# Attention maxima in blocks of 32 queries by 96 keys, with four head groups on the partitions, in a fused attention and expert layer

## The reference

```
q, k, v = split(x @ w_qkv.T)                       # 16 heads of 8 features
scores  = q k^T / sqrt(8)                          # allowed: j <= i and i - j < 64
x1      = layernorm(x + softmax(scores) v @ w_out.T + b_out)
logits  = x1 @ gate_w + gate_b; top 2 of 8 experts, softmax over the two
expert  = silu(((x1 w1 + b1) * (x1 w2 + b2)) wg + bg) w3 + b3
out     = layernorm(x1 + sum over the two of weight * expert(x1))
```

## Time and profile before

| what | value |
|---|---|
| time, median of 3 runs | 330.24 us (330.13 to 331.91) |
| the profiled execution's own time | 330.35 us |
| its span on the core | 328.4 us, mean granted PE clock 0.922 |
| PE | 254.0 us (77%), weight loads 175.7 us beside them |
| DVE | 252.1 us (77%) |
| POOL | 187.5 us (57%) |
| ACT | 148.1 us (45%) |
| spread, L960 | 64 x 754 ns = 48.2 us of DVE |
| find, L950 | 64 x 682 ns = 42.0 us of DVE |

### The profile page before, as it was taken

The page is one execution under the profiler, slowest core; times in us unless marked ns, Lnnn a source line. Parts: engine busy times, 40 slices in busy tenths (PEclk is TensorE's granted clock), DMA queues, the critical chain, the costliest instruction groups (busy, mean ns, idle before and its releaser), DMA issues.

```text
span 328.4 us, 7553 instructions
## 1 busy us (share of the span) xinstructions
PE 254.0 (77%) x1727; PEld 175.7 (53%) x1727; DVE 252.1 (77%) x707; ACT 148.1 (45%) x394; POOL 187.5 (57%) x292
## 2 busy tenths in 40 slices
PE   3486789799796979978758787799999999997000
PEld 1144566576565657656535554666677666675000
DVE  5699979999989999999674678577787777774091
ACT  3446365736555564654512563244443344433033
POOL 6849063777768777777765365224455555555251
PEclk9999799989799997999976999799999999999555
DMA  4643444476566677565623011221112111110432
GB/s 136 180 123 99 126 125 110 137 188 193 159 201 155 183 206 191 169 169 183 229 98 73 3 42 48 70 63 48 43 47 57 35 41 43 49 32 6 147 141 96
DMA packets 33987, 36.48 MB, mean 111 GB/s; under 512 B 4972, under 2 KB 30062, under 8 KB 33824
## 3 DMA queue, kind: packets, MB, share of 16 engines
q1 hardware_dynamic: 30864, 29.69, 31.9%
q0 software_dynamic: 2336, 4.37, 4.0%
q10 hardware_dynamic: 752, 2.03, 1.9%
HBM read 25.48 MB, written 11.05 MB: 111 GB/s over the span
## 4 chain that ended last, share of the span: by engine, by line
PE 43%; DVE 27%; issue 15%; DMA 5%; SPq 3%; ACT 3%; DVEq 2%; POOL 1%; ACTq 0%; POOLq 0%
PE bank L1541 9%; PE bank L1513 8%; DVE shift L960 6%; PE bank L1504 6%; DVE top L950 4%; PE bank L1339 2%; PE bank L1536 2%; PE bank L1341 2%; PE bank L1529 2%; PE bank L1358 2%; PE bank L1361 2%; PE bank L1375 2%; DMA w_up<-expert_out 1%; DMA expert_out<-probs,tile_x 1%; PE bank L1385 1%
## 5 line engine op out<-in xcount | busy, mean ns | idle before, releaser
L718 POOL DMA_INDIRECT expert_out<-probs,tile_x x39 | 40.5, 1039 | 58.0 <-DVE probs L1245 56.4
L816 ACT ACTIVATE probs<-bank 128x512 f32<-128x512 f32 x64 | 35.1, 595 | 52.8 <-PE bank L1361 52.8
L960 DVE TENSOR_TENSOR shift<-top,delta 64x512 fp32r<-64x512 f32 x64 | 48.2, 754 | 2.5 <-PE bank L1361 1.1
L667 POOL DMA_INDIRECT routed<-rows,place x32 | 34.3, 1073 | 21.8 <-issue 16.9
L950 DVE TENSOR_REDUCE top<-bank 128x4 f32<-128x512 f32 x64 | 42.0, 682 | 2.2 <-PE bank L1341 1.5
L1541 PE MATMUL bank<-w_up,x_unit 128*128 x78 | 42.3, 625 | 0.0
L1250 DVE TENSOR_TENSOR w_rows<-bank,b_up 128x512 f32<-128x512 f32 x39 | 26.9, 689 | 18.1 <-PE bank L1541 18.0
L1513 PE MATMUL bank<-w_gate,x_all 128*128 x156 | 40.3, 381 | 0.5 <-DVE v_aug L1236 0.5
L1504 PEld LDWEIGHTS bank<-w_down,xT 128*128 128x128 f32 x156 | 21.0, 193 | 32.2 <-issue 32.2
L1341 PE MATMUL bank<-k_slots,q_halves 128*128 128x512 f32 x64 | 37.5, 642 | 0.0
L889 ACT COPY x_unit<-bank 128x128 f32<-128x128 f32 x39 | 10.3, 264 | 53.8 <-PE bank L1521 53.8
(11 more groups left out here) (173 smaller groups left out, 563.9 us busy)
## 6 DMA issues: line engine op xcount, KB each, us to landing
k_stack<-k_scratch SPq DMA_DIRECT2D x28, 160.0 KB
q_stack<-q_scratch SPq DMA_DIRECT2D x62, 64.0 KB
tile_x<-routed SPq DMA_DIRECT2D x39, 65.0 KB, 1.8
k_scratch<-k_parts SPq DMA_DIRECT2D x7, 320.0 KB, 2.5
q_scratch<-q_parts SPq DMA_DIRECT2D x8, 256.0 KB, 2.2
w_up<-in_L_ffn_w_dram SPq DMA_DIRECT2D x16, 128.0 KB
w_gate<-in_L_ffn_wg_dram SPq DMA_DIRECT2D x8, 256.0 KB
b_up<-in_L_ffn_b_dram SPq DMA_DIRECT2D x2, 1024.0 KB
```

The source lines that it names most:

```text
L667: eng.indirect_dma_start(routed, bass.IndirectOffsetOnAxis(ap=place[i][:, k:k + 1], axis=0), rows[i][:, k, :], None, bounds_check=SPARE + ...
L718: eng.indirect_dma_start(expert_out, bass.IndirectOffsetOnAxis(ap=tile_x[i][:, P:P + 1].bitcast(I32), axis=0), y[i][:, :], None, bounds_ch ...
L816: eng.activation(probs[t[1] % 2][a][:, 512 * h:512 * h + 512], t_bank[h][:, :], ACT.Exp).then_inc(probs_ready, 1)
L960: eng.tensor_tensor(shift[a][half][r, :, :], top[a][r, :].unsqueeze(2).to_broadcast([64, 8, QT]), delta[r, :].unsqueeze(1).to_broadcast([6 ...
```

## The change

The maxima are now found in blocks of 32 queries. The 128 output partitions are 4 head groups x 32 queries, in place of 2 halves x 64 queries, and the columns are 4 slots x 96 keys (32 queries reach back 64 keys), in place of 8 slots x 128 keys in two banks. Bank h now belongs to the block of queries, no longer to the slots. So:

- ACT makes four masked copies of a unit's queries (`q_quarters`) in place of two, and no key slots.
- POOL makes all four key slots, with one instruction of 4 x 320 columns. Both banks wait for it (`slots_ready`).
- The mask matmul covers only the first and the last 32 of the 96 keys, 4 x 64 columns (all 384 for the first block of a sequence); its weights `rep_b` repeat an identity of 32 for the four groups.
- The score matmul and the find have 384 columns in place of 512.
- The spread writes 64 partitions x 256 elements in place of 512: a partition stands for one group and query, and holds 4 slots x 64 queries. Its operands now have four dimensions.
- The matmul that subtracts the maxima is split in two of 256 columns, each with its own weights: -1 in the rows of its own group, 0 in those of the other, and the mask in the other 64 rows.
- Constants are added at the start: a memset and two copies for `rep_b` on POOL, a reduction for `delta_block` and more, smaller fills of `shift_w` on DVE.

```diff
+QB = 32
+BLOCK_KEYS = WINDOW + QB
...
-        q_halves = [sb(f"q_halves{i}", [P, WIN, 2, QT], F32R) for i in range(2)]
-        k_slots = [sb(f"k_slots{i}", [P, 8, KEYS], F32R) for i in range(2)]
+        q_quarters = [sb(f"q_quarters{i}", [P, 2 * WIN, 4, QB], F32R) for i in range(2)]
+        k_slots = [sb(f"k_slots{i}", [P, 4, KEYS], F32R) for i in range(2)]
-        shift = [[sb(f"shift{a}{h}", [P, 8, QT], F32R) for h in range(2)] for a in range(2)]
+        shift = [[sb(f"shift{a}{h}", [P, 4, QT], F32R) for h in range(2)] for a in range(2)]
...
+            step(eng.memset(rep_b[:, :, :, :], 0.0))
+            for b in range(2):
+                r = slice(QB * b, QB * b + QB)
+                step(eng.tensor_copy(rep_b[r, b, :, :], ident_b[r, r].unsqueeze(1).to_broadcast([QB, 4, QB])))
...
-                eng.tensor_tensor(k_slots[i][:, 4:8, :],
+                eng.tensor_tensor(k_slots[i][:, :, :],
-                                  slot_col[:, 4:8].unsqueeze(2).to_broadcast([P, 4, KEYS]),
-                                  ALU.mult).then_inc(slots_high, 1)
+                                  slot_col[:, :].unsqueeze(2).to_broadcast([P, 4, KEYS]),
+                                  ALU.mult).then_inc(slots_ready, 1)
...
-                wait(eng, halves_ready, ucount(u, 2, 0))
+                wait(eng, quarters_ready, ucount(u, 4, 0))
-                for half in range(2):
-                    eng.activation(q_halves[i][:, :, half, :],
-                                   q_parts[:, 0, :].bitcast(F32).rearrange("p (w q) -> p w q", w=WIN),
-                                   ACT.Copy, scale=half_col[:, half:half + 1]).then_inc(halves_ready, 1)
+                for quarter in range(4):
+                    eng.activation(q_quarters[i][:, :, quarter, :],
+                                   q_parts[:, 0, :].bitcast(F32).rearrange("p (b q) -> p b q", q=QB),
+                                   ACT.Copy, scale=quarter_col[:, quarter:quarter + 1]).then_inc(quarters_ready, 1)
-                wait(eng, slots_high, ucount(u, 1, 0))
-                wait(eng, slots_low, ucount(u, 4, 0))
+                wait(eng, slots_ready, ucount(u, 1, 0))
-            def key_slots(u):
-                i = u[1] % 2
-                eng.wait_ge(k_hi, ucount(u, 1, 1))
-                wait(eng, s_filled, ucount(u, 8, -8))
-                for c in range(4):
-                    eng.activation(k_slots[i][:, c, :], k_parts[:, 0, :].bitcast(F32), ACT.Copy,
-                                   scale=slot_col[:, c:c + 1]).then_inc(slots_low, 1)
...
+            eng.tensor_reduce(quarter_col[:, :], head_of[:, :].rearrange("p (h g) -> p g h", h=4), AX_X,
+                              ALU.add).then_inc(dve_const, 1)
+            eng.tensor_reduce(slot_col[:, :], head_of[:, :].rearrange("p (h g) -> p h g", h=4), AX_X,
+                              ALU.add).then_inc(dve_const, 1)
+            eng.tensor_reduce(delta_block[:, :], ident[:, :].rearrange("p (b q) -> p q b", q=QB), AX_X,
...
-                    eng.memset(shift_w[r, half, :, :].bitcast(F32), -1.0).then_inc(shift_const, 1)
-                    eng.tensor_copy(shift_w[o, half, :, :], mask_f[o, :, :]).then_inc(shift_const, 1)
+                    for l in range(2):
+                        for own in range(2):
+                            g = 64 * half + QB * (l if own else 1 - l)
+                            eng.memset(shift_w[g:g + QB, half, l, :, :].bitcast(F32), -1.0 if own else 0.0).then_inc(shift_const, 1)
+                    eng.tensor_copy(shift_w[o, half, :, :, :],
+                                    mask_f[o, :, :].unsqueeze(1).to_broadcast([64, 2, 2, P])).then_inc(shift_const, 1)
-                                        delta[o, :].unsqueeze(1).to_broadcast([64, 8, QT])).then_inc(shift_const, 1)
+                                        delta[o, :].unsqueeze(1).to_broadcast([64, 4, QT])).then_inc(shift_const, 1)
...
-                                  s_bank[h][:, :].rearrange("p (s k) -> p s k", s=4), AX_X,
+                                  s_bank[h][:, 0:4 * BLOCK_KEYS].rearrange("p (s k) -> p s k", s=4), AX_X,
...
                     wait(eng, t_filled, count(t, 4, 2 * a + 2 - 4))
                     eng.wait_ge(s_read, count(t, 4, 2 * a + 2))
                 r = slice(64 * half, 64 * half + 64)
-                eng.tensor_tensor(shift[a][half][r, :, :], top[a][r, :].unsqueeze(2).to_broadcast([64, 8, QT]),
-                                  delta[r, :].unsqueeze(1).to_broadcast([64, 8, QT]),
+                eng.tensor_tensor(shift[a][half][r, :, :].rearrange("p s (b q) -> p b s q", b=2),
+                                  top[a][r, :].rearrange("p (b s) -> p b s", b=2).unsqueeze(3).to_broadcast([64, 2, 4, QB]),
+                                  delta_block[r, :].unsqueeze(1).unsqueeze(1).to_broadcast([64, 2, 4, QB]),
                                   ALU.mult).then_inc(shift_ready, 1)
...
-                wait(eng, halves_ready, ucount(u, 2, 2))
+                wait(eng, quarters_ready, ucount(u, 4, 4))
+                wait(eng, slots_ready, ucount(u, 1, 1))
-                    if h == 0:
-                        wait(eng, slots_low, ucount(u, 4, 4))
+                    at = QT * w + QB * h
+                    scores = s_bank[h][:, 0:4 * BLOCK_KEYS].rearrange("p (s k) -> p s k", s=4)
+                    masks = mask_q[:, first, QB * h:QB * h + BLOCK_KEYS]
+                    wait(eng, s_read, count(t, 4, 2 * a + h - 1))
+                    if first and h == 0:
+                        eng.matmul(scores, rep_b[:, h, :, :].rearrange("p g q -> p (g q)"),
+                                   masks.unsqueeze(1).to_broadcast([P, 4, BLOCK_KEYS]), start=True, stop=False,
+                                   skip_group_check=True)
-                        wait(eng, slots_high, ucount(u, 1, 1))
-                    wait(eng, s_read, count(t, 4, 2 * a + h - 1))
-                    eng.matmul(s_bank[h][:, :], ident_b[:, :], mask_q[:, first:first + 1, :].to_broadcast([P, 4, P]),
-                               start=True, stop=False)
-                    eng.matmul(s_bank[h][:, :], q_halves[i][:, w, :, :],
-                               k_slots[i][:, 4 * h:4 * h + 4, QT * w:QT * w + P],
-                               start=False, stop=True).then_inc(s_filled, 1)
+                        edges = [x.rearrange("p s (e k) -> p s e k", k=QB)[:, :, 0:3:2, :]
+                                 for x in (scores, masks.unsqueeze(1).to_broadcast([P, 4, BLOCK_KEYS]))]
+                        eng.matmul(edges[0], rep_b[:, h, :, :].rearrange("p g q -> p (g q)"), edges[1],
+                                   start=True, stop=False, skip_group_check=True)
+                    eng.matmul(scores, q_quarters[i][:, 2 * w + h, :, :].rearrange("p g q -> p (g q)"),
+                               k_slots[i][:, :, at:at + BLOCK_KEYS],
+                               start=False, stop=True, skip_group_check=True).then_inc(s_filled, 1)
-                    eng.wait_ge(shift_const, 10)
+                    eng.wait_ge(shift_const, 16)
...
                         eng.matmul(t_bank[h][:, 256 * l:256 * l + 256], k_stack[i][:, grp, QT * w:QT * w + P],
                                    q_stack[i][:, grp, :, QT * w:QT * w + QT], start=(l == 0), stop=False,
                                    skip_group_check=True)
-                    eng.matmul(t_bank[h][:, :], shift_w[:, h, first, :], shift[a][h][:, :, :], start=False,
-                               stop=True, skip_group_check=True).then_inc(t_filled, 1)
+                    for l in range(2):
+                        ins = eng.matmul(t_bank[h][:, 256 * l:256 * l + 256], shift_w[:, h, l, first, :], shift[a][h][:, :, :],
+                                         start=False, stop=(l == 1), skip_group_check=True)
+                    ins.then_inc(t_filled, 1)
```

More of the change, by code:

```diff
@@ L128, in moe_layer_program @@
         mask_q = sb("mask_q", [P, 2, P], BF16)
-        shift_w = sb("shift_w", [P, 2, 2, P], F32R)
+        rep_b = sb("rep_b", [P, 2, 4, QB], BF16)
+        shift_w = sb("shift_w", [P, 2, 2, 2, P], F32R)
         delta = sb("delta", [P, QT])
+        delta_block = sb("delta_block", [P, QB])
         below = sb("below", [P, P], BF16)
@@ L133, in moe_layer_program @@
         head_of = sb("head_of", [P, HEADS])
-        half_col = sb("half_col", [P, 2])
-        slot_col = sb("slot_col", [P, 8])
+        quarter_col = sb("quarter_col", [P, 4])
+        slot_col = sb("slot_col", [P, 4])
         expert_iota = sb("expert_iota", [P, E])
@@ L294, in moe_layer_program @@
         v_ready = sem("v_ready")
-        halves_ready = sem("halves_ready")
-        slots_low = sem("slots_low")
-        slots_high = sem("slots_high")
+        quarters_ready = sem("quarters_ready")
+        slots_ready = sem("slots_ready")
         q_out = sem("q_out")
@@ L614, in _ @@
                 eng.nop().then_inc(rows_free[i], 1)
-            eng.wait_ge(dve_const, 3)
```

(9 more changed lines are left out.)

## The result

The changed kernel took 320.38 us (median of 4 runs, 319.99 to 321.06) against 330.19 us for the kernel before on the same chip: a ratio of 0.9698, 95% interval 0.9664 to 0.9732. The forecast was 318.6 us.

A forecast was written before the change was run, and what follows sets the result against it. Prediction: DVE bounds the attention loop, POOL about half a microsecond a pair behind. Gains of 4.0 before slot 4, 6.0 in the loop and 1.8 in the tail, 11.8 us off 330.35, gave 318.6 us (range 311 to 326).

The forecast's parts named there:

- Spread and find: DVE in attention: each spread 0.26 us shorter, each find 0.13 us shorter, 1.56 us less a slot.
- Up to slot 4 DVE's shortening counts in full: Slots 1 to 3, where POOL has slack: 4.7 us plus a 1.45 us wait gone, less quarters and start; 4.0 us.
- The loop, 6.0 us at 17.55 a pair: Four pairs of slots from slot 4: POOL takes over, its stretched short instructions and waits shrink; 19.05 to 17.55 us a pair.
- DVE as the bound, POOL about half a microsecond a pair behind: Attention loop of the kernel before: DVE runs without gaps; POOL, waiting 0.56 us for mean_var in even slots, is just behind.
- The tail, 1.8 us: From k_slots of slot 12 to the rows of step 12: 21.18 us becomes 19.4, bounds 0 to 2.8 gained.
- Start, 0.3 late: Start of attention: added constants delay POOL by about 0.9 us, less two half spreads; 0.3 us late, bounds 0 to 1.5.
- PE's 0.6 us a slot, off the path: PE in attention: fewer mask and score columns save 0.7 us a slot, the split shift matmul costs 0.1; no time gained.
- Quarters cost nothing in the loop: ACT's four query copies add 0.91 us in odd slots ahead of o_raw; costed at nothing in the loop, as POOL bounds it.
- move as a block: The expert tiles after attention are unchanged, so they start 11 to 12 us earlier and take as long as before.
- the first fell: Rival: POOL doesn't take over, DVE's 1.56 us count in all of slots 1 to 14, 21.8 us: 308.5 us; chance 0.12.
- the second fell: Rival: POOL's short instructions stay as long, POOL saves only its waits, 3.2 us in the loop: 324.2 us; chance 0.20.
- the third fell: Rival: PE idles waiting for k_slots and its clock drops; at half share 1.1 us a slot lost: 340 us; chance 0.09.

The follow-up runs named there:

- the second: The changed kernel run once more, unedited, for a second set of runs and a second profile: 318.92 us, ratio 0.967.
- dve_short_alone: The kernel before with only DVE's two instructions shortened: find reads 96 of 128 keys, spread fills 4 of 8 slots; 318.89 us, ratio 0.9662.
- find_short_alone: The kernel before with find alone shortened, to 96 of the 128 keys of each slot: 326.07 us, ratio 0.9846.
- all_three: The changed kernel with two key slots by ACT, o_raw ahead of the queries, and PE kept busy before the last x1 transpose: 310.40 us, ratio 0.9392.
- o_raw_first: The changed kernel with ACT's o_raw copy moved ahead of the queries in odd slots: 319.38 us, ratio 0.9676.
- pool_half_us_more: The changed kernel with two more one-column instructions on POOL at the head of each normalise: 324.20 us, ratio 0.9832.

## Why the prediction was right, step by step

The forecast of 318.6 lies 1.8 us under the first median and 0.3 under the second. Its mechanism holds in the changed kernel: DVE's saving paid, and POOL sets the pair. Its sizes were off in terms that partly cancel. Attention won 12.95 us up to the rows of step 12, where 11.8 was forecast, and the tiles, put at no change, gave 2.6 of it back in the profiled execution; that the total lies so near is partly luck.

- **Spread and find** were priced at 0.26 and 0.13 us; they fell by 0.264 and 0.133. Right.
- **"Up to slot 4 DVE's shortening counts in full", 4.0 us:** 2.58. This is the step that failed most: what DVE saved went in good part into waiting for PE. POOL's k_slots of slot 2 starts at 42.66 against 42.96 before, so slot 1 gave 0.3 and not 1.56. First the old k_slots, then DVE's waits in slot 1 of the changed kernel:

```profile
42.96 2.54 POOL L622 TENSOR_TENSOR k_slots<-k_parts,slot_col 128x1280 fp32r<-128x1280 f32 x1 [10.70 <-ACT k_parts L794]
```

```profile
39.07 1.02 DVE L951 TENSOR_REDUCE top<-bank 128x4 f32<-128x384 f32 x2 [0.88 <-PE bank L1351]
40.68 0.26 DVE L975 RECIPROCAL o_den<-bank 128x16 f32<-128x16 f32 x1 [0.59 <-PE bank L1397]
41.62 0.87 DVE L961 TENSOR_TENSOR shift<-top,delta_block 64x256 fp32r<-64x256 f32 x2 [0.37 <-PE bank L1372]
```

  From 33.5 to 42.8 DVE was busy 6.85 us where it was 8.37, 1.52 less, but it waited 1.84 us for PE where it had waited 0.58. PE's granted clock in that stretch was 0.82 in both kernels. In dve_short_alone it was 1.00, and slot 1 gave 1.23; there slots 2 and 3 gave only 1.0, with one wait of 2.25 us for PE's scores. Its 2.2 at slot 4, without quarters, says that the 1.8 us set down to the quarters is not what was missing. How much of PE's lateness is the clock's was not tried.
- **The loop, 6.0 us at 17.55 a pair:** 7.56 at 17.17. The named cause is right, POOL's short instructions shrink. The term was mis-sized: 0.5 us a slot from L631 and L633 was 0.54 in fact, but L658 (0.20) and the scatters (0.05 each) shrank too, which the sum left out. The 0.5 a pair for the wait for mean_var did not come: 3.0 us of idle in four pairs became 2.5.
- **DVE as the bound, POOL about half a microsecond a pair behind:** the runs correct this. POOL's instructions were the same before and after, and the loop's gain is almost all in their durations. From find_short_alone on, each us off DVE paid only 0.5 to 0.7 us. So DVE did not hand over to POOL at one point. That POOL's series already paced much of the loop before, and that DVE's length entered it by stretching POOL and by the wait for mean_var (2.9 us in four pairs), is argued from these rows; no run lengthened POOL in the kernel before. The Trainium skill states a rule that fits this ("SBUF — State Buffer", SBUF: two separate sides): a DVE operation with two SBUF inputs and a GpSimd operation that reads SBUF exclude each other from a shared port pair, and whichever starts first has it for its whole instruction. The trace agrees both ways: L631 (now L638) fell from 571 to 257 ns with the spread halved, and DVE's L1032 took 2.21 us beside k_slots and 0.16 in an odd slot.
- **The tail, 1.8 us** (k_slots of slot 12 to the rows of step 12): 21.18 became 18.37, 2.8 and not 1.8: the late pace exactly, the upper bound.
- **Start, 0.3 late:** slot 1's find starts at 33.65 against 33.55. Right in kind.
- **PE's 0.6 us a slot, off the path:** dve_short_alone with the old matmuls and all_three with the new ones both ran at a granted 1.00 in the loop and PE was busy 60.1 and 56.8 us in four pairs: 0.4 a slot less. The forecast was 0.6, and off the path it is, since dve_short_alone is as fast without it. By the rule of the Trainium skill on weight loads that the prediction estimated from ("TensorE: Matmul & The Clock Gate", LDWEIGHTS (loading the stationary operand)) it would have been an estimated 0.2; the 0.4 lies between.
- **Quarters cost nothing in the loop:** right, by o_raw_first.
- **The tiles "move as a block":** they took 2.6 us longer in the first profile and 1.3 in the second. In the first it was the stretch behind the first w_up matmul, with the clock's lower level in it, which was not foreseen at this place; in the second the first w_up matmul came later (6.8 us after rest_row, against 5.4 in the first and 5.2 before).
- **What would show it:** k_slots 17.2 to 17.9 apart (17.17), L633 at 0.3 to 0.4 us (0.30) and the spread at 0.42 came. The DVE gaps ahead of a find, released by PE's scores, came ahead of the loop (0.88 us at 39.07) and not in it: there DVE waited 2.5 us for ACT's k_parts, 2.3 for PE ahead of the spread and 1.3 for the turn. In the loop PE waited for k_slots only in the runs with o_raw first. The expert tiles did start 11 to 12 us earlier and more (12.75 by the early table), but took longer.
- **The rivals:** POOL took over (17.0 is a floor), so the first fell; POOL's short instructions shrank, so the second fell; the granted clock in the loop was 0.95 against 0.93, so the third fell. (Its "f of about 0.12" is the share of time at the lower level; as the share of PE's work, which its formula takes, it is an estimated 0.06. Nothing hangs on it.)

## What to carry to other kernels

A busy share does not tell which engine sets a loop. Add half a microsecond to one engine and see whether the loop grows by it: here, in the changed kernel, POOL at 73% busy answered in full and DVE at 83% by a quarter. Where two engines hold each other up, as DVE and POOL here, shortening the one's instructions also shortens the other's, and a next step is to move work to a third engine, as two of the key slots to ACT.

## What was not expected of the hardware

- One spread more ahead of POOL's 4.7 us addition put split_keys behind it and moved slot 4 by 6.9 us: where an instruction stood at the start of this long hold counted for more than its length.
- PE's clock fell to 0.50 after a 2 us stretch with 0.33 us of work in one execution, and stayed at 1.00 after the same stretch in another execution of the same kernel (windows above). Of the twelve profiles without the added transposes three show the drop at this place: the first of the changed kernel, pool_half_us_more and o_raw_first. All are among the seven that start from the changed kernel, none among the kernel before and the four that start from it. What decides it among the seven stays open.
